# Attention blocks 8 to 14: probabilities turned by 32x32 squares, through DRAM and VectorE, instead of by TensorE

## The reference

```python
Q, K, V = (x @ Wq, x @ Wk, x @ Wv)
energy = jnp.einsum('bqd,bkd->bqk', Q, K)
...
energy = jnp.where(pad | causal, NEG_INF, energy)
score = jax.nn.softmax(energy / np.sqrt(DK), axis=-1)
return jnp.einsum('bqk,bkd->bqd', score, V)
```

## Time and profile before

| | |
|---|---|
| median of 3 runs | 1645.36 us (1645.16 to 1645.95) |
| the profiled execution | 1649.54 us, span 1647.7 us |
| TensorE busy | 1610.7 us, 98% |
| VectorE, ScalarE, GpSimd busy | 53%, 35%, 22% |
| self-attention, blocks 8 to 14 | 197.3 to 338.0 us (batch 0) and 507.4 to 648.0 us (batch 1) |
| chain that ended last | TensorE 85%, VectorE 6%, ScalarE 4% |

### The profile page before, as it was taken

How to read it: one execution, slowest core, us unless ns; L and a number is a source line. 1 busy time by engine, 2 the same in 40 slices (tenths; PEclk the granted TensorE clock), 3 DMA queues, 4 the chain that set the end, 5 groups by cost and what they waited for, 6 DMA issues and landing times.

```text
span 1647.7 us, 20596 instructions
## 1 busy us (share of the span) xinstructions
PE 1610.7 (98%) x7538; PEld 1323.5 (80%) x7538; DVE 876.6 (53%) x1784; ACT 572.6 (35%) x990; POOL 363.9 (22%) x562
## 2 busy tenths in 40 slices
PE   8999999999999999899999899999999999999999
PEld 6887888877788888677777688888888888888887
DVE  6757544477664444688888966333333332423311
ACT  5432121134222212466666544232323232333322
POOL 1212100022220000288888911000000000000000
PEclk9999999999999999799999999999999999999999
DMA  6302110131221104456664354111212111121100
GB/s 213 101 27 96 45 52 26 39 110 58 72 74 34 52 26 142 135 140 171 157 178 163 112 157 126 64 39 56 47 52 50 54 39 64 39 64 32 46 0 26
DMA packets 177161, 130.87 MB, mean 79 GB/s; under 512 B 121073, under 2 KB 121073, under 8 KB 176907
## 3 DMA queue, kind: packets, MB, share of 16 engines
q1 hardware_dynamic: 175264, 126.10, 25.9%
q10 hardware_dynamic: 1797, 3.46, 0.6%
HBM read 87.34 MB, written 42.18 MB: 79 GB/s over the span
## 4 chain that ended last, share of the span: by engine, by line
PE 85%; DVE 6%; ACT 4%; issue 2%; POOL 2%; DMA 0%; DVEq 0%; SPq 0%; ACTq 0%; POOLq 0%
PE banks L760 82%; PE banks L970 2%; ACT plain L1318 2%; DVE split L1697 1%; ACT split L1154 1%; PE banks L770 1%; DVE plain L2068 1%; ACT plain L1328 1%; DVE tile_x L2075 0%; DVE plain L2058 0%; DMA plain<-in_L_xattn_Wk 0%; POOL split L1572 0%; DVE plain L1836 0%; DVE split_q L1697 0%; POOL split L1579 0%
## 5 line engine op out<-in xcount | busy, mean ns | idle before, releaser
L760 PE MATMUL banks<-split_q,split 128*128 128x512 f32 x2328 | 565.8, 393 | 4.9 <-POOL split L1572 3.0
L760 PE MATMUL banks<-split 128*128 128x512 f32 (+5 forms) x2304 | 543.0, 385 | 8.3 <-DVE split L1697 5.9
L760 PEld LDWEIGHTS banks<-split_q,split 128*128 128x128 f32 x2328 | 434.1, 188 | 98.7 <-POOL split L1572 4.0
L760 PEld LDWEIGHTS banks<-split 128*128 128x128 f32 (+3 forms) x2304 | 414.8, 185 | 103.9 <-issue 8.2
L760 PE MATMUL banks<-split,split_q 128*128 128x512 f32 (+3 forms) x1728 | 393.2, 380 | 7.2 <-DVE split_q L1697 4.1
L760 PEld LDWEIGHTS banks<-split,split_q 128*128 128x128 f32 x1728 | 308.4, 189 | 60.3 <-DVE split_q L1697 4.9
L2216 DVE TENSOR_TENSOR split<-plain,split 128x512 fp32r<-128x512 f32 x128 | 88.5, 692 | 386.8 <-ACT split L1473 386.7
L1467 ACT ACTIVATE plain<-banks,small 128x512 f32<-128x512 f32 x128 | 88.3, 690 | 402.4 <-PE banks L760 402.4
L1697 DVE TENSOR_TENSOR split<-banks,split 128x512 fp32r<-128x512 f32 (+5 forms) x232 | 146.1, 637 | 149.4 <-ACT split L1154 149.1
L1154 ACT ACTIVATE split<-banks 128x512 fp32r<-128x512 f32 (+5 forms) x232 | 124.0, 555 | 244.5 <-PE banks L970 190.9
L1506 POOL TENSOR_TENSOR small<-small 128x1 f32<-128x1 f32 x64 | 13.1, 204 | 475.6 <-DVE small L1733 475.4
(11 more groups left out here) (157 smaller groups left out, 1265.3 us busy)
## 6 DMA issues: line engine op xcount, KB each, us to landing
plain<-in_x SPq DMA_DIRECT2D x64, 256.0 KB, 2.7
xo_scratch<-plain SPq DMA_DIRECT2D x32, 256.0 KB, 2.3
x_scratch<-plain SPq DMA_DIRECT2D x32, 256.0 KB, 2.0
plain<-x_scratch SPq DMA_DIRECT2D x32, 256.0 KB, 3.0
tile_x<-xo_scratch SPq DMA_DIRECT2D x32, 256.0 KB, 3.2
xg_scratch<-tile_x SPq DMA_DIRECT2D x32, 256.0 KB, 2.1
out<-plain SPq DMA_DIRECT2D x32, 256.0 KB, 2.1
plain<-xg_scratch SPq DMA_DIRECT2D x7, 1024.0 KB, 5.5
```

Source lines behind the costliest of these rows:

```text
L760: mm = nc.tensor.matmul(out, left(c, l), right(c, r), start=start and c == 0 and (l, r) == PASSES[0], stop=stop and c == chunks - 1 and (l ...
```

## The change

Blocks 8 to 14 (`turned`) don't use TensorE for T. After the exponential, SyncE stores each chunk of the row to DRAM (`store_p`) and reads it back with four DMAs that swap 32x32 squares (`load_p`), into the same place in `Srow`. VectorE then turns the squares while it writes the bank: a new step I(i, c). ScalarE's and VectorE's halves of T stay. The lists of these blocks are written anew; in a block of four chunks the order is A S0 S1 I0 T0 S2 I1 T1 B S3 X I2 V0 T2 I3 V1 T3 V2 V3, in which S and X are of block i + 1 and I, T, V of block i. SyncE's new work stands after the store of block i's result and serves block i + 2. Blocks 0 to 7 and 15 keep TensorE's transposes.

```diff
+def turned(i):
+    return 8 <= i < NB - 1
+
+def squares_in(b, i, c):
+    return sum(turned(j) and c < chunks_of(j) for j in range(NB)) * b + sum(
+        turned(j) and c < chunks_of(j) for j in range(i + 1))
...
         end = [(kind, i - 1, 0) for kind in "AB"]
-        if n1 > n0:
+        if turned(i) and n1 > n0:
+            g = i // 4 + 1
+            order += [("Q", g, 0), end[0], ("Q", g, 1), end[1], ("I", i, 0), ("I", i, 1), ("Q", g, 2), ("T", i, 0),
+                      ("Q", g, 3), ("T", i, 1), ("V", i, 0), ("I", i, 2), ("S", i + 1, 0), ("T", i, 2)]
+            order += [("S", i + 1, c) for c in range(1, n1)]
+            order += [("X", i + 1, 0), ("V", i, 1), ("V", i, 2)]
+        elif turned(i):
+            order += [end[0], ("S", i + 1, 0), ("S", i + 1, 1), ("I", i, 0), ("T", i, 0), ("S", i + 1, 2), ("I", i, 1),
+                      ("T", i, 1), end[1]]
+            order += [("S", i + 1, 3)] if n0 > 3 else []
+            order += [("X", i + 1, 0), ("I", i, 2), ("V", i, 0), ("T", i, 2)]
+            order += [("I", i, 3), ("V", i, 1), ("T", i, 3)] if n0 > 3 else [("V", i, 1)]
+            order += [("V", i, c) for c in range(2, n0)]
+        elif n1 > n0:
...
+                def store_p(i, c):
+                    n, at, w = squares_in(b, i, c), c * 512, width_of(i, c)
+                    if n > 1:
+                        sp.wait_ge(p_in[c], (n - 1) * QB * 16)
+                    sp.dma_start(p_dram[c, 0:P * w].rearrange("(p n) -> p n", n=w), Srow[:, i % 2, at:at + w]).then_inc(p_out[c], 16)
+
+                def load_p(i, c):
+                    at, w = c * 512, width_of(i, c)
+                    sp.wait_ge(p_out[c], squares_in(b, i, c) * 16)
+                    squares_of = p_dram[c, 0:P * w].rearrange("(q s c i r) -> i s c q r", q=QB, s=32, i=QB, r=32)
+                    for n in range(QB):
+                        sp.dma_start(Srow[32 * n:32 * n + 32, i % 2, at:at + w].rearrange(
+                            "p (c q r) -> p c q r", q=QB, r=32), squares_of[n]).then_inc(p_in[c], 16)
...
                     sp.dma_start(x1_dram[b * S + i * P:b * S + (i + 1) * P, :], U[:, i % 2]).then_inc(
                         x1_out[i % 2], 16)
+                    if turned(i + 2):
+                        sp.wait_ge(p_ready, b * NB + i + 2 + 1)
+                        for c in range(chunks_of(i + 2)):
+                            store_p(i + 2, c)
+                        for c in range(chunks_of(i + 2)):
+                            load_p(i + 2, c)
...
-                    elif kind == "T":
+                    elif kind == "T" and not turned(i):
                         n = TURNS["p", b, i, c]
                         if c == 0:
                             pe.wait_ge(p_ready, b * NB + i + 1)
+                        if c == 0 and turned(i - 1):
+                            pe.wait_ge(tp_full, n)
...
+                    elif kind == "I":
+                        n, at, w = TURNS["p", b, i, c], c * 512, width_of(i, c)
+                        dve.wait_ge(p_in[c], squares_in(b, i, c) * QB * 16)
+                        dve.wait_ge(tp_free, n + 1)
+                        nc.vector.transpose(PS[:, 2 + n % 2, 0:w], Srow[:, i % 2, at:at + w]).then_inc(tp_full, 1)
```

More of the change, by code:

```diff
@@ L169, in turns_of_attention @@
         for kind, i, c in ORDERS[b]:
-            if kind == "T":
+            if kind == ("I" if turned(i) else "T"):
                 order.append(("p", b, i, c))
@@ L255, in build @@
         xg_dram = nc.dram_tensor("xg_scratch", (B * S, E), F32, kind="Internal").ap()
+        p_dram = nc.dram_tensor("p_scratch", (C, P * 512), F32, kind="Internal").ap()
         h_dram = nc.dram_tensor("h_scratch", (TILE, E), F32, kind="Internal").ap()
@@ L438, in build @@
         h_out, hb_in = sem("h_out"), sem("hb_in")
+        p_out, p_in = [sem(f"p_out_{c}") for c in range(C)], [sem(f"p_in_{c}") for c in range(C)]
         block = ctx.enter_context(nc.Block())
```

## The result

| | before | after |
|---|---|---|
| median of 5 runs | 1645.95 us (1645.16 to 1650.59) | 1657.67 us (1656.96 to 1659.62) |
| ratio, with its 95% interval | | 1.0065 (1.0048 to 1.0083) |
| the profiled execution | 1649.54 us, span 1647.7 | 1659.62 us, span 1657.8 |

The account below looks back on a forecast made before the run. The order of TensorE's own work was taken as the bound. Per batch, 10.1 us removed against 14 of waiting gave +3.85, +7.7 in all; GpSimd +3.0 made +10.7 on 1645.36: 1656 us, range 1643 to 1669.

Parts of the forecast that it names:

- TensorE's saving: Blocks 8 to 14: 84 transposes a batch taken off TensorE, 0.12 us each, 10.1 us a batch, 20.2 in all.
- The chain: VectorE and ScalarE steps before V0, V1, V2 in blocks 8 to 14 come late: 14 us of waiting a batch.
- the links: Step times and hand-offs in blocks 8 to 14, each from a profile row; summed +3.85 us a batch, +7.7 in all.
- Block 11: Block starting with the next four query products: V0 at 12.9 us instead of 10.9, block length 30.3 us.
- GpSimd's place: GpSimd's row operation prolongs VectorE's B in blocks 13 and 14: 0.75 us each, +1.5 a batch, +3.0 in all.
- The squares: DMA reloads before VectorE's transposes land in time: taken as 0; about +20 us if each landing needed 3 us more.
- The rival of the late squares: VectorE waits for the DMA before I0 and all queued behind moves along: 1662 to 1676 us; chance 0.15.
- The clock: Rival: one stretch of 20 us in each batch at TensorE's lower clock, about +20 us, 1676; chance 0.05.
- The sum: Blocks 8 to 14 of both batches +7.7 us, GpSimd next to B +3.0: +10.7 in all, 1656 us.

Follow-up runs that it names:

- the lists by chunk: The changed kernel with other lists: each chunk turned directly behind the next block's score chunk, last score and X ahead of B; 1640.4 us, ratio 0.996.
- that of blocks 8 to 11 alone: The changed kernel with the change in blocks 8 to 11 only, 12 to 14 keeping TensorE's transposes and old lists; 1655.35 us, ratio 1.0048.
- the run above: The changed kernel with SyncE's row store and row load moved between the second and third chunk's squares; 1658.16 us, ratio 1.0061.
- the run with both edits: The lists by chunk, plus SyncE's row store and row load between the second and third chunk's squares; 1639.73 us, ratio 0.9952.

## Why the prediction was right

- **TensorE's saving.** TensorE's own pace is as summed: the 48 score matmuls of block 12 took 9.59 us from start to start (277.17 to 286.76) against the 9.7 of the sum. With 130.6 us of work a batch and the clock's 1.7 and 3.1 us, 15.4 and 14.6 us are left for waits (14 were forecast). No run measures a transpose alone; 0.12 us is what 140.7 leaves over 130.6.
- **The chain.** Block 8's V0 at 8.69 (8.64), block 12's V2 at 17.17 (17.4): the links, each from a row, added up within 0.25 us wherever GpSimd was not in the way, block 11 apart. The waits the trace names, 12.1 us in batch 0, are less than the 14 to 15 because each modelled end of a matmul covers a part of its gap. Moving B and doubling a transpose confirmed two links by their size.
- **Block 11 was mis-sized.** I took B(10) as prolonged there as before and V0 at 12.9. The row load now came later, B was free, and V0 started at 11.63: the block took 29.0 instead of 30.3.
- **GpSimd's place was wrong, its size nearly right.** Predicted: 0.75 us in each of blocks 13 and 14, +3.0. Shown: six prolonged operations of B in after. Five (225.43, 242.09, 309.83, 557.90, 649.03 us) are longer by 0.6 to 0.9 us each, in blocks 9, 10 and 13 of batch 0 and 10 and 14 of batch 1, the sixth (333.22, block 14 of batch 0) by 0.25: 4.4 together. Blocks 9 and 10 took 1.0 and 0.8 longer than summed in batch 0. But moving the load gave nothing back: in these lists the meetings are a cost that shifts with the schedule.
- **The squares.** In time, as taken: no wait at a transpose. The landing stayed at the 2.4 us of the earlier trace rows. The rival of the late squares did not come, in this order of the lists; in the lists by chunk it did, at 3.0 us at most (batch 1).
- **The clock was mis-sized.** I had priced it as one stretch of 20 us at the lower level in each batch, rare. It came in three bites of 1.5 to 1.7 us. The ground for the low chance was that TensorE would be busy about 18.5 of 20 us (the sum itself gives 18.1, the window of after 18.4), near a row at full clock; the falls came all the same. In the sum this stood at nothing; it is 4.7 us of the profiled execution, and is the largest term that is missing. Block 11 saved 2.7 us, which hides a part of it.
- **The sum.** +10.7 predicted, +11.7 measured by medians. The stretches alone are +14.4 in the profiled execution: 7.7 from the links, 4.7 from the clock, and 2 that are left between GpSimd's meetings (+4.4) and block 11 (-2.7). Against the stretches the forecast was 3.7 us short, for want of the clock term. That the total came closer than this is luck, as far as the two profiles tell: errors of opposite sign in block 11 and the clock, and 4 us that the profiled executions give back around 700 us, where no term of the sum lies.

## What to carry to other kernels

Work taken off the engine that bounds the time is won only if the chain that replaces it ends, link by link, before that engine asks: VectorE was busy half of the time and still set the time one for one. Such a chain could be added up from rows to 0.25 us where no other engine interfered, and the order of the list decides it: the same operations cost 12 us in one order and won 6 in another, by turning each chunk right behind its score and by keeping the operations that nobody waits for, here B, out of the way. Where waits of about 2 us appear in TensorE's row, count more than the waits themselves: behind 12 of the 20 waits of 1.95 us or more in these runs the clock fell, for some 1.5 us each.

## What the runs showed of the hardware that was not expected

- A wait of about 2 us in a stretch that is else without gaps can bring TensorE to its lower clock for about 3 us: 4.3 to 4.6 us for twelve matmuls of 512 columns instead of 3.0. In blocks 8 to 14 of after and of the runs (that of blocks 8 to 11 alone left out) it followed 12 waits: four of 1.95 us, and those of 2.01, 2.08, 2.09, 2.41, 2.42 (twice), 2.83 and 2.85. It did not follow eight others: three of 1.95 us, and those of 2.17, 2.20, 2.28, 2.54 and 2.65; nor any shorter one. Waits of the same length in the same kernel had it and had not (1.95 us, in after), so the length alone does not decide. What does stays open.
- GpSimd's row operation and VectorE's B, or the last part of its score, take turns side by side, and the rows tell how. At 224.80 GpSimd starts during L1788 (till 225.39) and takes 0.45 us more than its 1.29. L1790 starts at 225.43 and ends at 227.09, 0.75 us after 226.34, about where GpSimd ends (226.54). At 242.09 VectorE starts second and alone loses. This is the exclusive lock of which the Trainium skill tells (SBUF — State Buffer, "SBUF: two separate sides"), and the trace agrees; the prediction had doubted it. The exception: where both start within 0.05 us (256.68 in the run above, and the earlier trace rows), it was VectorE that waited, though its record starts no later. So it was too at 515.22 in the lists by chunk and at 558.86 in the run with both edits, 0.01 us apart (1.85 us instead of 0.75). VectorE's transposes into the bank and its remainders, which read the bank, ran beside GpSimd at their usual 0.72 and 0.69 us.
- A DMA of 32x32 squares into 32 partitions takes SyncE about 0.65 us to issue (four in 2.6 us), so a block of four chunks keeps its queue for 11 us (sixteen in 10.99 us in after, from 277.44 on), and whatever stands behind, here the row load, moves with it.
